# Both loads of x from arrays laid out per partition, residual rows with odd and even columns apart

## The reference, cut to what matters

```python
x_ft = jnp.fft.rfftn(x, axes=(-2, -1))                       # first step, x = _gn(x)
blk = jnp.einsum('bimn,hiomn->bhomn', x_ft[:, :, :32, :32], weight)
xr = jnp.fft.irfftn(out_ft, s=(64, 64), axes=(-2, -1))       # out_ft: blk in the low modes, else 0
x = x + jnp.einsum('bchw,oc->bohw', xr, fc_w) + fc_b

pooled = x.mean(axis=(2, 3))                                 # second step, x = _gn(x)
att = softmax(sigmoid(pooled @ ksm_w.T))                     # 16 weights per image
kernels = clip(ifft2(einsum('bk,koihwc->boihwc', att, dft_weight)).real, -10, 10)
x = x + (conv3x3(x, kernels, one set per image) + bias) * fbm_scale
```

## Time and profile before

| what | us |
| --- | --- |
| median of three runs | 136.77 |
| the three runs | 136.77, 135.37, 137.23 |
| the profiled execution's own time | 136.2 |
| its span in the trace | 134.3 |
| PE busy | 122.4 (91% of the span) |
| DVE busy | 87.9 (65%) |
| ACT busy | 71.2 (53%) |
| POOL busy | 53.5 (40%) |
| share of PE in the chain that ended last | 82% |

### The profile page before, as it was taken

One profiled execution on the slowest core, in us unless ns is written; L12 is line 12 of the kernel. 1 busy time (PEld: TensorE's weight loads), 2 busy tenths in 40 slices (PEclk: granted clock), 3 DMA queues, 4 the chain that ended last, 5 costly groups with the idle time before them and its releaser, 6 DMA issues.

```text
span 134.3 us, 3911 instructions
## 1 busy us (share of the span) xinstructions
PE 122.4 (91%) x1608; PEld 92.8 (69%) x1608; DVE 87.9 (65%) x195; ACT 71.2 (53%) x143; POOL 53.5 (40%) x46
## 2 busy tenths in 40 slices
PE   0787999999999999999999979979999999999960
PEld 0777999999999889999999968943322523233330
DVE  0068798689999925644377677999946699633240
ACT  0387676558965645433167656728988059302200
POOL 7995000019969999999911900504000000000000
PEclk9999999999999999999999999999999999999998
DMA  3999999999800067878786989779989888784467
GB/s 81 248 248 259 262 254 328 286 394 403 315 7 10 11 154 179 197 166 192 169 192 149 170 153 177 187 179 176 205 172 171 189 189 187 172 196 92 103 145 150
DMA packets 71921, 25.24 MB, mean 188 GB/s; under 512 B 67936, under 2 KB 68192, under 8 KB 71904
## 3 DMA queue, kind: packets, MB, share of 16 engines
q1 hardware_dynamic: 70816, 24.73, 78.1%
q10 hardware_dynamic: 1088, 0.26, 1.0%
HBM read 14.50 MB, written 4.19 MB: 139 GB/s over the span
## 4 chain that ended last, share of the span: by engine, by line
PE 82%; DVE 6%; DMA 3%; SPq 3%; issue 3%
PE slot L1070 28%; PE slot L983 11%; PE slot L998 9%; PE slot L903 8%; PE slot L924 8%; PE slot L972 5%; PE slot L958 4%; DMA x_buf<-x 3%; PE aggp L1028 3%; PE small L924 1%; PE aggp L924 1%; SPq L313 1%; DVE x_buf L674 1%; DVE q_buf L686 1%; SPq L308 1%
## 5 line engine op out<-in xcount | busy, mean ns | idle before, releaser
L1070 PE MATMUL slot<-w_buf,conv_w 128*32 128x512 f32 (+1 forms) x136 | 31.8, 603 | 0.0
L1070 PE MATMUL slot<-y_buf,conv_w 128*32 128x512 f32 (+1 forms) x136 | 31.7, 603 | 0.0
L903 PE MATMUL slot<-cst,x_buf 128*128 128x128 f32 x128 | 16.9, 292 | 5.5 <-DMA x_buf<-x 5.5
L903 PEld LDWEIGHTS slot<-cst,x_buf 128*128 128x128 f32 x128 | 16.1, 206 | 5.8 <-issue 4.6
L1070 PEld LDWEIGHTS slot<-w_buf,conv_w 128*32 128x32 f32 x136 | 9.5, 109 | 11.6 <-issue 10.9
L839 DVE TENSOR_TENSOR bd_buf<-slot,q_buf 128x512 f32<-128x512 f32 (+1 forms) x17 | 10.8, 658 | 9.5 <-PE slot L1070 9.3
L998 PE MATMUL slot<-cst,t_buf 128*128 128x128 f32 x128 | 15.5, 278 | 0.8 <-issue 0.8
L632 DVE TENSOR_REDUCE row_sq<-q_buf 128x16 f32<-128x1024 f32 (+1 forms) x9 | 9.8, 1097 | 9.2 <-ACT q_buf L478 9.1
L998 PEld LDWEIGHTS slot<-cst,t_buf 128*128 128x128 f32 x128 | 14.7, 192 | 1.4 <-issue 1.2
L460 POOL TENSOR_TENSOR x_buf<-y_buf 128x1024 f32<-128x1024 f32 x4 | 7.7, 1938 | 18.9 <-DVE y_buf L727 18.9
L983 PE MATMUL slot<-cst,r_buf 128*64 128x128 f32 x256 | 14.6, 274 | 0.0
(11 more groups left out here) (125 smaller groups left out, 218.0 us busy)
## 6 DMA issues: line engine op xcount, KB each, us to landing
x_buf<-x SPq DMA_DIRECT2D x36, 128.0 KB, 3.1
w_buf<-w_modes SPq DMA_DIRECT2D x16, 256.0 KB, 5.5
w_buf<-y_buf SPq DMA_DIRECT2D x16, 256.0 KB, 6.0
x_buf<-x SPq DMA_DIRECT2D x14, 256.0 KB, 4.4
out<-bd_buf SPq DMA_DIRECT2D x28, 128.0 KB, 2.9
t_buf<-dft_w SPq DMA_DIRECT2D x4, 288.0 KB, 6.6
t_buf<-x_buf SPq DMA_DIRECT2D x8, 128.0 KB, 3.0
r_buf<-x_buf SPq DMA_DIRECT2D x8, 128.0 KB, 3.3
```

Source lines behind the costliest of these rows:

```text
L903: last = pe.matmul(ps[:, col:col + 128], x_part(k)[:, 4 * j + i].rearrange("p q w -> p (q w)"), const("fwd_h"), start=True, stop=True)
L1070: last = pe.matmul(ps[32 * j:32 * j + 32, 32 * u0:32 * u1], cw[r][:, b, k, :], src, start=(k == terms[0][0]), stop=(k == terms[-1][0]))
```

## The change

The host hands over x twice: `x_cols`, in which each of the eight parts is an array of 128 partitions by 1024 floats in the order in which SBUF holds it, and `x_rows`, in which each image is an array of 128 partitions by 1024 floats, each image row with its odd columns first and then its even ones. A load then takes 512 floats of a partition that lie together (first load, two for each part, by halves of the channels and no longer by image) or 1024 (second load, one for each image). The second load waits for all nine counts of `mix_done` ahead of its first image. The inverse transform `inv_w` gives its columns in the same order, so that `xa` and `xb` hold pad, 32 columns, 32 columns, pad: the even and the odd columns of the padded row, each kind together. `columns_from` takes 32 columns that lie together where the kernel before took every second one; `conv` and POOL's sum use it. What is computed is the same.

```diff
+BY_PARITY = np.r_[1:W:2, 0:W:2]
...
-        a[0, y, :, y] = weight * np.cos(th * np.outer(m, h))
+        a[0, y, :, y] = weight * np.cos(th * np.outer(m, BY_PARITY))
...
+        def columns_from(rows, col):
+            at = (col % 2) * (W // 2 + 1) + col // 2
+            return rows[..., at:at + W // 2]
...
-        def load_rows(eng, k, q):
-            b, c0 = 2 * (k // 2) + q, 16 * (k % 2)
-            eng.dma_start(x_part(k)[:, :, q, :], x[b, c0:c0 + 16].rearrange("(c x) h w -> (x h) c w", x=2)
-                          ).then_inc(xh_in[2 * k + q], 16)
...
+        def load_part(eng, k, j):
+            at = 1024 * k + 512 * j
+            eng.dma_start(x_buf[:, at:at + 512], x_cols[k, :, 512 * j:512 * j + 512]).then_inc(xh_in[2 * k + j], 16)
...
             sp.wait_ge(f1_done, 16)
             sp.wait_ge(sq_ready, 9)
+            sp.wait_ge(mix_done, 9)
             for b in (0, 2, 1, 3, 4, 6, 5, 7):
-                if b in (0, 4):
-                    sp.wait_ge(mix_done, 6 if b == 0 else 9)
-                for j in range(4):
-                    sp.dma_start(xr[32 * j:32 * j + 32, b],
-                                 x[b].rearrange("c (u j) w -> j c u w", j=4)[j]).then_inc(xr_in[2 * (b // 4) + b % 2], 16)
+                sp.dma_start(x_buf[:, 1024 * b:1024 * b + 1024], x_rows[b]).then_inc(xr_in[2 * (b // 4) + b % 2], 16)
...
-                    nc.gpsimd.tensor_tensor(sa[:, bs], xa[:, bs, :, 1:W + 1:2], xa[:, bs, :, 2:W + 2:2],
+                    nc.gpsimd.tensor_tensor(sa[:, bs], columns_from(xa[:, bs], 1), columns_from(xa[:, bs], 2),
...
-                    if k == 0:
-                        pe.wait_ge(xh_in[j], rows_landed(0))
-                    elif j == 0:
-                        pe.wait_ge(xh_in[2 * k], rows_landed(k))
-                        pe.wait_ge(xh_in[2 * k + 1], rows_landed(k))
+                    pe.wait_ge(xh_in[2 * k + j], 16)
...
-                            src = (xb if shifted else xa)[:, b, u + u0:u + u1, col:col + W - 1:2]
+                            src = columns_from((xb if shifted else xa)[:, b, u + u0:u + u1], col)
```

More of the change, by code:

```diff
@@ L83, in constants @@
     for y in range(2):
-        a[0, y, :, y] = weight * np.cos(th * np.outer(m, h))
-        a[1, y, :, y] = -weight * np.sin(th * np.outer(m, h))
+        a[0, y, :, y] = weight * np.cos(th * np.outer(m, BY_PARITY))
+        a[1, y, :, y] = -weight * np.sin(th * np.outer(m, BY_PARITY))
     put("inv_w", a)
@@ L104, in constants, with spectral_then_attention_conv @@
     return out.astype(np.float32)
-def spectral_then_attention_conv(nc, x, w_modes, dft_w, params, consts, out):
+def spectral_then_attention_conv(nc, x_cols, x_rows, w_modes, dft_w, params, consts, out):
     with ExitStack() as ctx:
@@ L330, in _ @@
             sp.dma_start(cst[:, 0:128], consts[:, 0:128]).then_inc(fwd_h_in, 16)
[L331 to L336, removed]
+            for k in range(8):
+                for j in range(2):
+                    load_part(sp, k, j)
                 if k == 1:
@@ L467, in copy_y, with square_x @@
                 act.activation(*y_part(k, 0), ACT.Copy).then_inc(y_act, 1)
-            def square_x(k, *qs):
-                sq, src = x_squares(k), x_part(k)
-                for q in qs:
-                    act.wait_ge(xh_in[2 * k + q], rows_landed(k))
-                if len(qs) == 1:
-                    sq, src = sq[:, :, qs[0]], src[:, :, qs[0]]
+            def square_x(k, *js):
+                cs = slice(4 * js[0], 4 * js[-1] + 4)
+                for j in js:
+                    act.wait_ge(xh_in[2 * k + j], 16)
+                sq, src = x_squares(k)[:, cs], x_part(k)[:, cs]
                 if k >= 2:
@@ L625, in copy_y, with sum_squares @@
                 nc.vector.tensor_copy(*y_part(k, 1)).then_inc(y_dve, 1)
-            def sum_squares(k, q=None):
+            def sum_squares(k, j=None):
                 sq, dst = x_squares(k), row_sq[:, k // 2, 8 * (k % 2):8 * (k % 2) + 8]
-                if q is not None:
-                    sq, dst = sq[:, :, q], dst[:, :, q]
-                v.wait_ge(sq_ready, k + 1 + (q or 0))
+                if j is not None:
+                    sq, dst = sq[:, 4 * j:4 * j + 4], dst[:, 4 * j:4 * j + 4]
+                v.wait_ge(sq_ready, k + 1 + (j or 0))
                 nc.vector.tensor_reduce(dst, sq, AX_X, ALU.add).then_inc(sq_used, 1)
@@ L843, in _ @@
             for k in range(4):
-                v.wait_ge(xr_in[k // 2], 128)
+                v.wait_ge(xr_in[k // 2], 32)
                 add_x(k)
@@ L855, in _ @@
             attention(0)
-            v.wait_ge(xr_in[2], 128)
+            v.wait_ge(xr_in[2], 32)
             add_x(4)
@@ L861, in _ @@
             kernel_sums(0)
-            v.wait_ge(xr_in[3], 128)
+            v.wait_ge(xr_in[3], 32)
             add_x(6)
@@ L1183 @@
     modes = modes.reshape(128, 4, 4, 512).transpose(1, 2, 0, 3)
-    arrays = {"x": array("x"), "w_modes": np.ascontiguousarray(modes), "dft_w": array("L1_conv_dft_weight"),
+    x = array("x")
+    cols = x.reshape(4, 2, 2, 8, 2, H, W).transpose(0, 2, 4, 5, 3, 1, 6).reshape(8, 128, 1024)
+    rows = x[..., BY_PARITY].reshape(B, C, UB, 4, W).transpose(0, 3, 1, 2, 4).reshape(B, 128, 1024)
+    arrays = {"x_cols": np.ascontiguousarray(cols), "x_rows": np.ascontiguousarray(rows), "w_modes": np.ascontiguousarray(modes), "dft_w": array("L1_conv_dft_weight"),
               "params": np.tile(params, (4, 1)), "consts": constants()}
```

## The result

The changed kernel took 135.37 us, the median of 20 runs, and the kernel before 136.64 in 20 runs beside them. The ratio is 0.9905 with a 95% interval of 0.9881 to 0.9928: 1.0 to 1.6 us were gained, where 4.2 had been forecast. The profiled execution took 135.21 us with a span of 133.3, against 136.2 and 134.3.

The account below looks back on a forecast made before the run. Bound by a start waiting for DMA and a last third where PE only steps through rounds. Terms -2.0 (start) and -2.2 (convolution) gave -4.2, from 136.5 to 132.3 us; range 130.2 to 134.8.

Parts of the forecast that it names:

- First load, starting PE: Start of kernel: PE's first 256 KB of x land sooner, PE starts at 3.65 us; about -0.5 us.
- the loads are not faster: Rival, start: something other than piece length holds it, only the convolution gains; 134.3 us, chance 0.10.
- First load, waits of PE: Start: waits for x ahead of `f1(1)` and `f1(2)` vanish, `f1(2)` starts at 8.85 us; -1.3 us.
- the 0.66 us for each 256 KB: First load: landing time per 256 KB of x at 399 GB/s, against 1.05 us at 250.
- The 16 instructions of `f1(0)`: Start of PE: said to take 3.36 us, 0.21 us each, all at half rate; duration kept after the change.
- the slower rival: Start: PE's half rate lasts longer, 0.1 us more per instruction of 128 columns; up to 139.5 us, chance 0.04.
- The reading of the convolution: Convolution: reading floats that lie together saves 0.039 us a round over 64 rounds; -2.2 us taken.
- taken whole: Convolution: all 0.039 us a round between 0.467 and 0.428 counted as gain, 2.5 us before covers.
- The row without gaps: Convolution: rounds without gaps, 0.428 us each, taken as nearest to the new reading.
- The second load (0): First four images' loads move behind `mix`, some 2.5 us later, with 18 us cover; no effect, 0.
- The rest (0): POOL's sums, squares, copies, pads, stores and the end: no effect on time, 0.

Follow-up runs that it names:

- matmuls of ones: Kernel after plus eight matmuls of ones, results unread, ahead of the first part of x: 133.84 us, ratio 0.9826; other runs put them on other kernels.
- later_sums: Kernel after with GpSimd's second to fourth sums moved to where VectorE has no step with both inputs in SBUF: 134.18 us, ratio 0.9853.

## Why the prediction was wrong

*First load, starting PE (-0.5 forecast, none found).* This step failed. The first load was to land sooner because its pieces are longer. The issue did get shorter (four take 1.84 us in place of 2.07). But the first one landed 2.90 us after its issue, at 4.11, where the two that PE waited for before had landed at 3.53 and 4.02, and PE started at 4.24 us; with the new load it started between 4.14 and 5.18 us in the eight profiled executions without matmuls of ones, with the old one at 4.15 and 4.46. The rate between 4 and 8 us is 246 to 287 GB/s, close to the 250 of the earlier trace rows; over 400 came only after 10 us. I had taken the rate of a stretch deep in the program, 28 to 34 us, for the start of it. For the first loads the rival "the loads are not faster" was right: something else than the length of the pieces holds them, and no run shows what.

*First load, waits of PE (-1.3 forecast).* This failed by the same term, the 0.66 us for each 256 KB. Part 2 was to be in by 7.5 us, at 300 GB/s by 8.9; it landed at 9.11 and 9.82. `f1(2)` could not have started at 8.85, and started at 9.91. The waits went, as said, but in part because PE came later to the data than forecast: the half rate was misread too. "The 16 instructions of `f1(0)`" were not all at half rate: in the trace of before, the starts lie 0.213 us apart for 13 of them and 0.111 from 7.01 us on. After the change 20 instructions ran at half rate, and 17 to 26 in the other executions with the new load, at 0.10 us each; the piece took 9.41 us, and 9.09 to 10.09 in the others, against 3.36 + 1.84 + 3.85 = 9.05 by the prediction. So the slower rival's mechanism took part, with 4 to 13 instructions (0.4 to 1.3 us) more at half rate than before; with two traces of the old load (13 and 15 instructions) it is not shown that the new load is its cause. Together the two steps gave 1.05 us in the profiled execution and 0.8 by the times, where 2.0 stood.

*The reading of the convolution (-2.2 forecast, -1.5 found).* Mechanism right, size off. Eight rounds fell from 3.75 to 3.53 us (106.91 to 110.44): 0.441 a round, 0.026 saved in place of the 0.039 "taken whole". The row without gaps was the wrong neighbour for the odd starts. The trace has the convolution at 38.97 in place of 40.46. The rule of the Trainium skill ("SBUF — State Buffer", "Door 1: The DMA port swizzle") that two hits in a line of 16 bytes are enough is not borne out for these reads, now that the same tile was read in both ways: 0.467 us a round with every second float, 0.43 where the floats lie together and begin even.

*The second load (0).* Right: `add_x` still waits 1.37 us for PE.

*The rest (0).* This is the step that cost most. "POOL's sums read nearer columns, but they wait for DVE and the convolution began on DVE's weights": the sums read columns that lie farther from each other, and DVE made those weights only when POOL let it. Each sum grew by 0.48 us. The two that run back to back ahead of `i2(4)` made VectorE 0.95 later, of which 0.61 reached `i2(4)`; the step on `kern` took 0.48 more; 1.08 us in all. later_sums, with sums as long and none of it lost, shows that the wait alone is the cause.

The sum by the chain: front -1.05, `f2` to `fc` +0.15, sums +1.08, convolution -1.49, together -1.31 behind the last matmul (129.78 to 128.47), where -2.0, 0, 0 and -2.2 stood.

## What to carry to other kernels

A change of layout for one reader is a change for all readers: list every instruction that reads the tile, on every engine, and price each anew. When an engine off the critical path gets slower, look for steps of its neighbour that end exactly when it ends; an idle-looking 0.9 us for 128x4 numbers was that sign, and it stood in the trace of before. A transfer rate holds for the stretch in which it was read: the 399 GB/s of 28 to 34 us said nothing of the first 8. And a wait for data in the first microseconds can hide a slow clock: take away the one, and the other is what remains.

## What was not expected of the hardware

GpSimd's addition of 128x1024 floats takes 1.92 us when its operands lie one float apart, in steps of one float as of two, and 2.40 when they lie 32 apart, in steps of one. VectorE's steps with two inputs in SBUF stretch from 0.16 to as much as 1.92 us beside it. A matmul that reads rows of 32 floats pays 0.02 to 0.03 us more per round of four when the rows begin at an odd float. With one and the same first load PE starts on x between 4.14 and 5.18 us, and 17 to 26 of its instructions run at half rate; with the two, the end of `f1(3)` varies from 13.64 to 14.98 us, as much as the front gained. From 4 to 8 us the loads move 246 to 287 GB/s in pieces of 2 KB, little more than the 216 to 269 in pieces of 256 bytes.
